# A three-layer graph network: means taken off on the chip, squares on ScalarE, one turning product per step

## The reference

```
h   = relu(layernorm(x))                      # ahead of layers 1 and 3
u   = h h' / sqrt(384);  a = softmax(u)
attn = a*adj / (sum(a*adj) + 1e-10)
ctx = upper(attn) @ (h Wl' + bl) + diag(attn) * (h Ws' + bs) + lower(attn) @ (h Wr' + br)
mean, var = ctx.mean(-1), ctx.var(-1)
h   = relu((ctx - mean) / sqrt(var + 1e-12) * gamma + beta)
x   = x + h                                   # behind layers 2 and 3
```

## Time and profile before

| | us |
|---|---|
| median of 3 runs (lowest, highest) | 1233.54 (1233.14, 1233.68) |
| the profiled execution | 1233.29 |
| its span, first to last instruction | 1231.5 |
| TensorE busy | 1215.2 |
| VectorE busy | 1089.2 |
| ScalarE busy | 833.1 |
| GpSimd busy | 326.8 |

### The profile page before, as it was taken

One profiled execution on the slowest core, in us unless ns is written; L12 is line 12 of the kernel. 1 busy time (PEld: TensorE's weight loads), 2 busy tenths in 40 slices (PEclk: granted clock), 3 DMA queues, 4 the chain that ended last, 5 costly groups with the idle time before them and its releaser, 6 DMA issues.

```text
span 1231.5 us, 26747 instructions
## 1 busy us (share of the span) xinstructions
PE 1215.2 (99%) x7163; PEld 1208.6 (98%) x7163; DVE 1089.2 (88%) x3127; ACT 833.1 (68%) x2079; POOL 326.8 (27%) x439
## 2 busy tenths in 40 slices
PE   7899999999999999999999999999999999999997
PEld 6899999999999999999999999999999999999997
DVE  6799888888887799999999999999999999999986
ACT  6577767666666667776766666676666666676764
POOL 1234232222222123321212121232323232323221
PEclk9999999999999999999999999999999999999999
DMA  5444232324232234333333323322332323232321
GB/s 179 135 121 129 89 114 83 118 82 119 83 106 91 94 99 130 116 100 104 96 106 96 107 85 103 129 85 95 97 107 98 106 95 99 96 97 98 99 91 54
DMA packets 112922, 127.18 MB, mean 103 GB/s; under 512 B 11104, under 2 KB 100192, under 8 KB 112864
## 3 DMA queue, kind: packets, MB, share of 16 engines
q1 hardware_dynamic: 112864, 126.50, 32.8%
HBM read 76.91 MB, written 49.55 MB: 103 GB/s over the span
## 4 chain that ended last, share of the span: by engine, by line
PE 97%; DMA 1%; issue 1%; DVE 1%; SPq 0%; ACT 0%; POOLq 0%; POOL 0%; DVEq 0%; ACTq 0%
PE right_bank L448 25%; PE left_bank L448 24%; PE context_bank L448 24%; PE context_bank L479 17%; PE score_bank L423 6%; PE score_bank L431 1%; DMA rows<-weights 1%; DMA nodes<-squares 0%; PE edge_bank L438 0%; ACT side_parts L610 0%; DVE context L872 0%; SPq L340 0%; DVE rows L881 0%; DVE stats L844 0%; DVE turned L744 0%
## 5 line engine op out<-in xcount | busy, mean ns | idle before, releaser
L448 PE MATMUL left_bank<-weight,node_t 128*128 128x384 f32 x1728 | 338.1, 339 | 0.0
L448 PE MATMUL right_bank<-weight,node_t 128*128 128x384 f32 x1728 | 335.0, 338 | 2.2 <-DVE weight L827 2.2
L448 PE MATMUL context_bank<-weight,node_t 128*128 128x384 f32 x1728 | 332.3, 337 | 3.1 <-ACT context_bank L616 3.1
L610 ACT ACTIVATE side_parts<-right_bank 128x384 fp32r<-128x384 f32 x192 | 94.4, 492 | 317.3 <-PE context_bank L479 317.1
L448 PEld LDWEIGHTS context_bank<-weight,node_t 128*128 128x128 f32 x1728 | 303.0, 188 | 3.7 <-ACT context_bank L616 3.4
L448 PEld LDWEIGHTS left_bank<-weight,node_t 128*128 128x128 f32 x1728 | 304.3, 188 | 0.0
L448 PEld LDWEIGHTS right_bank<-weight,node_t 128*128 128x128 f32 x1728 | 299.4, 188 | 3.5 <-issue 2.6
L479 PE MATMUL context_bank<-side_parts,attn_t 128*128 128x386 f32 x1152 | 240.0, 344 | 2.2 <-issue 1.9
L479 PEld LDWEIGHTS context_bank<-side_parts,attn_t 128*128 128x128 f32 x1152 | 198.9, 189 | 4.5 <-issue 3.6
L748 DVE TENSOR_TENSOR node_t<-nodes,node_t 128x768 fp32r<-128x768 f32 x94 | 121.6, 1294 | 18.2 <-ACT node_t L558 18.2
L1034 POOL TENSOR_TENSOR edge_block<-edge,tri 128x512 f32<-128x512 f32 x96 | 131.9, 1374 | 0.0
(11 more groups left out here) (78 smaller groups left out, 1519.6 us busy)
## 6 DMA issues: line engine op xcount, KB each, us to landing
squares<-turned SPq DMA_DIRECT2D x94, 384.0 KB, 2.7
nodes<-squares SPq DMA_DIRECT2D x376, 96.0 KB, 2.2
rows<-x SPq DMA_DIRECT2D x64, 384.0 KB, 3.7
out<-rows SPq DMA_DIRECT2D x31, 384.0 KB, 2.6
adj_in<-adj SPq DMA_DIRECT2D x96, 64.0 KB, 1.9
piece<-weights SPq DMA_DIRECT2D x18, 192.0 KB, 2.5
rows<-weights SPq DMA_DIRECT2D x3, 576.0 KB, 8.5
vector_rows<-vectors SPq DMA_DIRECT2D x3, 384.0 KB, 5.3
```

What stands on the lines that cost most here:

```text
L448: mm = nc.tensor.matmul(bank[:, 0:D], node_t[:, s.parity, k, c, a], weight[:, s.phase % 2, w, c, b], start=False, stop=(c, a) == (CH - 1, ...
L610: nc.scalar.activation(side_parts[:, side, HI, 0:D], side_bank[side][k][:, 0:D], ACT.Copy).then_inc(side_hi[side], 1)
```

## The change

In phases two and three (for all steps but the very last, `Step.level`) the context has mean zero, because ScalarE takes the row means off: `split_piece` makes one pass over a weight piece that sums it (scale -1/384) and one that adds the sum back while rounding; `level_bias` does the same to the bias rows. The low part of a piece is now VectorE's, one piece per step in steps 3 to 11, and the bias rows are levelled in steps 28 to 30. `walk` writes out twelve steps ahead of the loop where it wrote eight. VectorE no longer takes context statistics there; `centre` is a product with gamma alone; ScalarE squares the context in place and sums it (`square`), and `spreads` waits for that. In every step of all phases the cross scores are packed by four copies into one 128x128 operand, turned by one product into `edge_bank`, and added by VectorE in one more addition (`add_cross`).

```diff
+    def level(self):
+        return self.phase > 0 and self.ahead(1).exists()
...
-PIECES_IN = {3: 2, 4: 2, 5: 2, 6: 2, 7: 1}
+PIECES_IN = {g: 1 for g in range(3, 3 + PIECES)}
+BIAS_IN = {PAIRS - 4: RIGHT, PAIRS - 3: LEFT, PAIRS - 2: SELF}
...
-        for half in range(first, first + 4):
+        for half in range(first, first + 6):
...
             def turn_cross(s):
-                pe.wait_ge(cross_copied, s.n + 1)
-                for k in range(2):
-                    mm = nc.tensor.matmul(score_bank[:, k * 256:k * 256 + P], cross[:, k], ident_r[:, :],
-                                          start=False, stop=True, skip_group_check=True)
-                mm.then_inc(cross_turned, 1)
+                pe.wait_ge(cross_packed, 4 * (s.n + 1))
+                at_least(pe, cross_added, s.n)
+                nc.tensor.matmul(edge_bank[:, 3 * P:4 * P], cross_pack, ident_r[:, :],
+                                 start=True, stop=True, skip_group_check=True).then_inc(cross_turned, 1)
...
             def copy_cross(s):
                 act.wait_ge(scored, s.n + 1)
+                at_least(act, cross_turned, s.n)
                 at_least(act, score_summed, 2 * s.n)
-                nc.scalar.activation(cross[:, :, :], scores4[:, :, 1, :], ACT.Copy).then_inc(cross_copied, 1)
+                for h, half in enumerate(HALVES):
+                    nc.scalar.activation(cross_here[h], scores4[half, :, 1, half], ACT.Copy).then_inc(cross_packed, 1)
+                for h, half in enumerate(HALVES):
+                    nc.scalar.activation(cross_blocks[HALVES[1 - h], 1 + h], scores4[half, 1 - h, 1, half], ACT.Copy).then_inc(cross_packed, 1)
...
             def seed_self(s, k):
                 bias_row_here(s, k, SELF)
-                at_least(act, centred, s.tile(k) - 1)
+                prev = s.ahead(-1)
+                if prev.exists() and prev.level():
+                    act.wait_ge(squared, prev.tile(k) + 1 - 2 * PAIRS)
+                else:
+                    at_least(act, centred, s.tile(k) - 1)
...
+            def square(s, k):
+                act.wait_ge(centred, s.tile(k) + 1)
+                act.wait_ge(spread_done, s.n)
+                nc.scalar.activation(context_bank[k][:, 0:D], context_bank[k][:, 0:D], ACT.Square, scale=float(D) ** -0.5,
+                                     accum_out=moments[:, k, 1:2]).then_inc(squared, 1)
...
             def sum_scores(s):
-                dve.wait_ge(cross_turned, s.n + 1)
+                dve.wait_ge(cross_packed, 4 * (s.n + 1))
...
+            def add_cross(s):
                 dve.wait_ge(cross_turned, s.n + 1)
+                dve.wait_ge(score_summed, 2 * s.n + 2)
+                nc.vector.tensor_tensor(score[:, :, :], score[:, :, :], turned_cross, ALU.add).then_inc(cross_added, 1)
...
             def spreads(s):
-                dve.wait_ge(moments_done, s.tile(2))
+                if s.level():
+                    dve.wait_ge(squared, s.tile(2) - 2 * PAIRS)
+                else:
+                    dve.wait_ge(moments_done, s.tile(2))
```

133 lines of the change are left out of this document (97 added, 36 removed).

## The result

The changed kernel takes 1242.32 us (median of 6 runs, 1241.64 to 1245.17), against 1233.14 us (6 runs, 1230.82 to 1233.68). The ratio is 1.009, with a 95% interval of 1.0079 to 1.01. It is 9 us slower, where 11 us faster was forecast. The profiled execution has a span of 1239.8 us against 1231.5.

A forecast was written before the change was run, and what follows sets the result against it. TensorE, busy 99%, was taken as the bound. Terms -13.0 (turning product), +1.0 (weight pieces) and +0.6 (tail) gave -11.4 us, so 1221.9 profiled and 1222.1 median; forecast 1219.5 to 1225 (chance 0.60), range 1219 to 1231.

The forecast's parts named there:

- The turning product: TensorE, every step: one of two products goes, worth 0.135 us (0.11 to 0.16), 13.0 us over 96 steps.
- The copies: ScalarE, cross scores: four copies hold the queue 0.66 us instead of 0.28, 1.07 without overlap; covered by idle time, cost nothing.
- Does a wait reach TensorE?: Series to the left split, counted in phase three: slack of 0.2 us becomes about 0.5, TensorE waits for nothing, cost zero.
- the signs of being wrong: Weighing's fourth product late; step 12.5 us or more in phases two or three; phase one cut by only 0.08 or 0.16.
- F: Experiments' theory, phase two: many small delays share 0.6 us slack; removing any one gives most of the loss back.
- A2: Experiments' rival theory, phase two: the moved product, with the squares or alone, is enough for the loss; 1246 to 1250 us.
- Statistics off VectorE: VectorE, phases two and three: two statistics and aggregates go, at least 0.8 us less per step; worth nothing by itself.
- Weight pieces: 18 pieces, two ScalarE passes and a 0.6 us VectorE difference: 0 to 7 us in all, taken as 1.0.
- The tail: Last step's first norm waits for square, spread and power: +0.6 us at the end (0 to 1).
- More steps written out: More steps written out instead of looped: hidden under idle time, 0.
- The function table: ScalarE squares might need their own table, over a hundred us; ruled out because the changed program has one load.
- Rival 1: Left split late, 63 steps in phases two and three: 0.26 us each, 16 us, 1238 (0.12); small overshoot 1228 (0.11).

The follow-up runs named there:

- Experiment three: Kernel before with only the new turning: four packing copies, one product, one more addition, statistics still on VectorE; 1241.26 us, ratio 1.0068.
- experiments four: Changed kernel with squares on ScalarE in phase three only; phase two keeps VectorE statistics and the gamma product's old place; 1231.37 us, 0.9988.
- experiment one: Changed kernel with the product with gamma of tile 0 behind the shift again in phase two; 1228.64 us, ratio to before 0.9977.
- Experiment eight: Kernel before with only tile 0's mean subtraction and gamma product put ahead of the shift in phase two; 1243.73 us, 1.0091.
- Experiment five: Changed kernel, phase two: gamma product behind the shift, ScalarE order exponential, scaling, left seed; 1225.69 us, 0.9943.
- experiment six: Changed kernel with the old turning: one copy, two turning products, two additions; squares and levelled rows stay; 1242.72 us, 1.0079.
- Experiment eleven: Changed kernel, gamma product behind shift and seed last in phase two, 24 steps written out per phase, late phase-two input statistics moved; 1223.38 us, 0.993.
- experiment seven: Changed kernel with 24 steps of each phase written out ahead of the loop instead of 12; 1239.74 us, 1.0061.
- nine: Changed kernel with ScalarE's left seed last in phase two, gamma product left ahead of the shift; 1232.73 us, 0.9999.

## Why the prediction was wrong, point by point

**The turning product: right in kind, a little large.** Forecast 0.135 us, bounds 0.11 and 0.16. Measured 12.47 - 12.35 = 0.12 us a step, in phase one and in the written-out steps of phase three, and in phase two from 12.59 to 12.47 where nothing waits. Over 96 steps that is 11.5 us instead of 13.0. Half of the pair's 0.27 was too much. The reading from a single product put into a projection, 0.11 us, was nearer. By the 81 ns of the Trainium skill (TensorE: Matmul & The Clock Gate, Back-to-back issue gap) the step would have become an estimated 12.39 us; it became 12.35, so the rows decided rightly.

**The copies: mis-sized.** Forecast: they hold ScalarE for 0.66 us, 1.07 at most. Measured from the first copy's start to the next instruction's: 699.36 - 698.41 = 0.95 us. The row of 0.28 us to the next start was for one copy of 256 columns over all partitions; the four small ones come 0.24 us apart on average, so a piece of a quarter of the size costs nearly as much as the whole. The forecast took 0.10 us of overlap off each; in the trace the second pair starts at 699.00, 0.02 behind the end of the first (698.98), and only the seed behind the last copy overlaps it. The Trainium skill (VectorE: DVE Perf Modes, The TRN2 errata) gave an estimated 0.89 us one behind the other; it was close, and the trace does not bear out my reason to set it aside. In phase two copies and added addition cost 0.17 us a step by experiments three and four (12.64 against 12.47).

The forecast asked what the copies delay on ScalarE, and not when the turning product wants them. Before, the copy ended 0.92 us ahead of that product. Now the fourth ends 0.25 ahead of it (1017.19 and 1017.44, phase three), and 1017.44 is still on time. In every second looped step ScalarE is late: its scaling stands at 1028.12 to 1028.65, the copies start 1.09 us behind the start of the scores instead of 0.99, the fourth ends at 1029.62, and the turning product comes at 1029.92, about 0.1 us late.

**Does a wait reach TensorE? This is the step that failed, and it failed by its choice of path and phase.** The series was counted to the end of the left split in phase three, and there it was right: forecast 1.5 us behind the projection's start, measured 1.47 and 1.70 in turn, both ahead of the 2.06 at which it is wanted, and the weighing starts at 1.56 without a wait. Order of time of the kernel after, phase three:

```profile
1009.40 1.73 PE L472 MATMUL right_bank<-weight,node_t 128*128 128x384 f32 x9
...
1010.32 0.55 DVE L911 TENSOR_TENSOR side_parts<-left_bank,side_parts 128x384 fp32r<-128x384 f32 x1
...
1010.96 1.21 PE L503 MATMUL context_bank<-side_parts,attn_t 128*128 128x386 f32 x6
```

For phase two no chain was counted; it was carried over from phase three. But phase two has instructions there that phase three has not: the shift, one exponential over 128 columns at the end of the step, and the scaling queued behind that and the seed on ScalarE. The weighing's first product waits for the scaled self part. This chain had 0.6 us of slack, and the change put 0.92 us into it: the product with gamma ahead of the shift, the longer copies, and the squares with what waits for them, less a statistic. The product's place is 0.47 of it by experiment one, where the shift starts 0.13 ahead of the projection again; how the rest divides was not measured. Experiment eight shows that the product's place alone makes the kernel 11.7 us slower (1243.73 - 1232.03, the kernel before measured beside it); experiment one shows that undoing it alone gives 13.7 us back. Experiment five takes the seed out of the same chain and comes to 1225.7, 3.6 us over the forecast. So the mechanism is settled: in phase two, shift to scaling to weighing. The move of the product was in the diff and in the orders that I read. I gave its new place no cost and did not ask what stands behind it on VectorE's queue in phase two. Of the signs of being wrong that the prediction named, the long step of phase two beside a short one of phase one came; the fourth product late behind the left split did not.

**How the causes share the 14.7 us is not additive.** From the steps: the place costs 0.46 us in a looped step on top of the rest (12.94 and 13.17 against 12.48 and 12.70), and 0.31 and 0.44 on the kernel before. Place and squares without the copies cost 0.21 and 0.34 (experiment six), less than the place alone. F was too weak: experiment eight was near its rival, since one delay alone was enough to use up the slack. But A2 alone does not hold either: over the step without a wait (12.47, or 12.59 with the old turning) the change loses 0.47 and 0.70 us, and without the copies 0.26 and 0.36 less.

**Statistics off VectorE: forecast as worth nothing, and worth something in both phases.** In phase two it is 2.7 us by experiments four and one (409.5 against 406.8), and experiments eight and six have the same sign (417.0 against 414.4, with other steps written out and other pieces). Experiment three shows that the turning without this relief costs phase three 5.4 us over the kernel before (392.3 against 386.9) by the late left split, where the full change gains 2.9. I had given this work no value; it is what pays for the added addition.

**Weight pieces: mis-sized.** Forecast 1.0 us in all. The steps with pieces grew from 12.77 to 13.33 each, and there are eight instead of four: 8 x 0.86 = 6.9 us over the step without a wait (12.47), against 4 x 0.18 = 0.7 before. Part of that is the late chain, which plain steps pay too (12.76 just ahead of them). With the chain repaired (experiment five) they take 12.62, 0.15 above their neighbours. The forecast's size is right only with slack.

**The end of phase two.** The last three steps, with the input statistics for phase three between the additions of the scores, went from 13.14 to 13.58. I did not mention them. Experiment eleven's 12.67 shows that this was a loss in the kernel before as well.

**The tail.** From the last turning product (at 1207.77 and 1215.86) to the end of the span: 23.73 before, 23.98 after. +0.25, forecast +0.6.

**More steps written out: cost nothing, right; the loop does.** The loops' cost of 0.12 us in two steps appears as soon as the slack is used up. It cost 8 x 0.12 = 1 us in phase three, where it is the turning product that comes late behind the copies, as above; I had counted no cost of a loop at all.

**The function table: right.** One load in the whole program. **The rivals.** Rival 1 named the right kind of thing (durations in a row, small slack) but the wrong wait and the wrong phase; its own overshoot of 0.26 us in 63 steps gave 16 us and 1238. Phase two alone lost 14.7 us and, besides, the 3.8 that its saved products were worth, 18.5 in all.

## What to carry to other kernels

Count the slack of every wait that an engine at 99% has in a step, in each kind of step by itself, before and after the change; the one that was last before is not the one that is last after, and a phase with more slack on one path may have less on another. When an instruction changes its place on a queue, ask for each instruction that it passes who waits for that one, even if the moved one costs half a microsecond and the engine is idle a tenth of its time. Where a step has a few tenths of slack, a wait costs more than its overshoot, so an edit that only restores the order (experiment one, 13.7 us) can be worth more than the product that the change saves.

## What the runs showed of the hardware

- **Small copies do not get cheaper side by side.** Two of 64 partitions x 128 columns and two of 64x64 hold ScalarE for 0.95 us, where one of 128x256 held it for 0.28. The second pair of the four starts 0.02 us behind the end of the first; nothing of them overlaps there.
- **A late wait costs TensorE more than its lateness.** In experiment eight the self part was 0.14 us late, and the step 0.31 and 0.44 longer in turn. The weighing starts 0.05 us behind the scaling's end in one step and 0.21 in the next, and the six products take 1.16 and 1.15 us to the next start instead of 1.05. In experiments one and nine a scaling that ended 0.06 us ahead of the weighing's place (1.50 against 1.56) still moved it to 1.71.
- **A hardware loop costs time only where there is no slack.** 12.36 us written out against 12.35 and 12.47 in turn looped in phase three (12.77 against 12.95 and 13.17 in phase two, experiment seven). In the kernel before the difference is 0.01 at most. In phase three it is ScalarE that is seen late, by 0.1 us at the copies in every second looped step; what makes it late is not shown.
